# The four loads of layer 1's x become a part of their own in a batch's first step, and the parts of the order stand otherwise

## The reference

```python
xn = layer_norm(x)
q, k, v = xn @ Wq + bq, xn @ Wk + bk, (xn @ Wv + bv) * mask
# layer 0: q = softmax over a head's channels, k = softmax over tokens
y = q @ (k.T @ v)                      # per head
# layer 1:
att = softmax(q @ k.T + (1 - mask) * -1e6, over the keys)
y = att @ v                            # per head
# both:
scale, shift = split(silu(cond) @ W_emb + b_emb)
h = layer_norm(y) * (1 + scale) + shift
x = x + silu(h) @ W_out + b_out
```

## Time and profile before

| | |
|---|---|
| median of three runs | 1425.0 us (1422.28 to 1427.76) |
| profiled execution | 1417.49 us, its span 1415.7 us |
| TensorE busy | 1335.9 us (94%) |
| VectorE, ScalarE, GpSimd busy | 1025.7, 783.6, 771.5 us |
| mean granted clock of TensorE | 0.98 of 2.4 GHz |
| waits of TensorE for a stack | 24.9 us in 22 |

### The profile page before, as it was taken

The page is one execution under the profiler, slowest core; times in us unless marked ns, Lnnn a source line. Parts: engine busy times, 40 slices in busy tenths (PEclk is TensorE's granted clock), DMA queues, the critical chain, the costliest instruction groups (busy, mean ns, idle before and its releaser), DMA issues.

```text
span 1415.7 us, 27902 instructions
## 1 busy us (share of the span) xinstructions
PE 1335.9 (94%) x10720; PEld 1064.4 (75%) x10720; DVE 1025.7 (72%) x2006; ACT 783.6 (55%) x1357; POOL 771.5 (54%) x692
## 2 busy tenths in 40 slices
PE   6899999999999899899999999999999999999888
PEld 4678888888888687577777777776777777777666
DVE  5788878788787876778757757657757757857755
ACT  4355455454554644656755755655755655665642
POOL 0323244332443425468667757748847847856963
PEclk9999999999999999999999999999999999999987
DMA  9021111321213376736436535535635645543602
GB/s 337 2 68 60 38 63 35 97 60 38 66 37 101 96 224 183 212 113 197 133 120 182 147 121 160 161 106 154 190 106 142 180 128 142 169 138 113 187 9 82
DMA packets 83301, 173.40 MB, mean 122 GB/s; under 512 B 7624, under 2 KB 7624, under 8 KB 83168
## 3 DMA queue, kind: packets, MB, share of 16 engines
q1 hardware_dynamic: 83168, 171.62, 40.9%
HBM read 104.45 MB, written 67.14 MB: 121 GB/s over the span
## 4 chain that ended last, share of the span: by engine, by line
PE 59%; DMA 15%; DVE 12%; ACT 6%; SPq 3%; issue 2%; POOL 2%; DVEq 0%; ACTq 0%; POOLq 0%
PE ps L511 11%; PE ps L513 10%; PE ps L512 10%; DMA Ks<-mask_scratch 9%; PE ps L668 7%; PE ps L685 6%; DMA Ks<-stack_scratch 6%; PE ps L726 5%; DVE cT L1188 4%; PE ps L506 4%; ACT ps L784 2%; ACT xTh L782 2%; PE ps L703 2%; PE ps L599 1%; PE ps L620 1%
## 5 line engine op out<-in xcount | busy, mean ns | idle before, releaser
L1363 POOL TENSOR_TENSOR Pb<-Pb 128x512 f32<-128x512 f32 x376 | 470.9, 1292 | 232.4 <-PE ps L726 226.4
L1188 DVE TENSOR_REDUCE cT<-ps 128x1 f32<-128x512 f32 x512 | 325.8, 685 | 134.2 <-PE ps L668 132.1
L926 ACT ACTIVATE Pb<-ps 128x512 f32<-128x512 f32 x512 | 285.8, 599 | 237.5 <-PE ps L685 227.0
L668 PE MATMUL ps<-Ks,Qs 98*128 98x512 f32 x512 | 192.2, 422 | 27.4 <-DMA Ks<-stack_scratch 13.0
L685 PE MATMUL ps<-Qs,Ks 106*128 106x512 f32 x512 | 200.0, 421 | 6.3 <-DVE xTl L1040 3.2
L668 PEld LDWEIGHTS ps<-Ks,Qs 98*128 98x128 f32 x512 | 97.8, 196 | 70.0 <-issue 23.4
L685 PEld LDWEIGHTS ps<-Qs,Ks 106*128 106x128 f32 x512 | 96.9, 192 | 52.2 <-issue 12.9
L1314 POOL TENSOR_TENSOR vt<-vt,qmx 128x512 f32<-128x512 f32 x32 | 33.7, 1055 | 168.2 <-DVE qmx L1105 168.2
L1286 POOL TENSOR_TENSOR rs<-ve,mhalf 128x4 f32<-128x4 f32 x32 | 33.0, 1031 | 156.0 <-DVE ve L1013 126.7
L511 PE MATMUL ps<-xTh,Wh_k 128*128 128x512 f32 x256 | 106.4, 416 | 3.5 <-DVE xTl L1040 2.4
L511 PE MATMUL ps<-Wh_o,sTh 128*128 128x512 f32 x256 | 106.3, 415 | 0.0
(11 more groups left out here) (173 smaller groups left out, 2977.3 us busy)
## 6 DMA issues: line engine op xcount, KB each, us to landing
Qs<-stack_scratch SPq DMA_DIRECT2D x32, 768.0 KB
Ks<-stack_scratch SPq DMA_DIRECT2D x32, 768.0 KB
stack_scratch<-sg_q SPq DMA_DIRECT2D x32, 512.0 KB, 2.7
stack_scratch<-sg_k SPq DMA_DIRECT2D x32, 512.0 KB, 3.0
wr<-in_x SPq DMA_DIRECT2D x32, 256.0 KB, 5.0
x_scratch<-wr SPq DMA_DIRECT2D x32, 256.0 KB, 2.2
stack_scratch<-sg_q SPq DMA_DIRECT2D x32, 256.0 KB, 3.1
stack_scratch<-sg_k SPq DMA_DIRECT2D x32, 256.0 KB, 3.5
```

The lines of the kernel that those rows point to most:

```text
L668: e.matmul(bank[:], Qs[par][0:RX, j, t * 128:(t + 1) * 128], Ks[par][0:RX, j, :], start=True, stop=True).then_inc(s["S"], 1)
L926: e.activation(p_buf(n, m)[:, j, :], ps[bank_of["a", n, m, j]][:], ACT.Exp).then_inc(s["P"], 1)
L1188: e.tensor_reduce(nx[:, n % 2, j, t, 0:1], ps[bank_of["S", n, j, t]][:], AX.X, ALU.max, negate=True).then_inc(s["S_max"], 1)
L1363: e.tensor_tensor(acc[:, j, :], acc[:, j, :], p_buf(n, m)[:, j, :], ALU.add).then_inc(s["Ps_pool"], 1)
```

## The change

The x loads leave `ae` and become the part `lx`, in the first step (g = 0) of the next batch, with marks 0.3 to 0.4. The wait is the same. Besides, many marks of `PLAN` differ, in layer 0 too; of those the diff shows a few.

```diff
-    "0v": ((0.523, 1.2), (0, 0.596)),
+    "0v": ((0.691, 1.2), (0, 0.596)),
...
-    "pv": ((0.365, 0.753, 0.853), (0.338, 0.879, 0.882), (0.466, 1.021, 1.054), (0.328, 0.788, 0.951)),
+    "pv": ((0.365, 0.753, 0.853), (0.338, 0.788, 0.879), (0.466, 1.021, 1.054), (0.328, 0.788, 1.006)),
...
+    "lx": ((0.3, 0.4), None, None, None),
...
+        if g == 0 and b and more:
+            put("lx", [("lx", 8 + b + 1)])
...
-            def ae(i, n):
-                b, g = divmod(n, NG)
-                if g == NG - 1 and b + 2 < B:
-                    e.wait_ge(s["PV"], 4 * n + 4)
-                    for t in range(4):
-                        e.wait_ge(s[f"st{t}"], 16 * (b + 3))
-                    load_x(8 + b + 2)
+            def lx(i, x):
+                e.wait_ge(s["PV"], 16 * (x - 9))
+                for t in range(4):
+                    e.wait_ge(s[f"st{t}"], 16 * (x - 7))
+                load_x(x)
```

More of the change, by code:

```diff
@@ L31 @@
     "st": (0.65,), "sta": (0.0,), "y": (0.3, 0.5, 0.45, 0.45),
-    "qk": MM + (0.3, 0.0), "stack": (0.0,),
+    "qk": MM + (0.3, 0.0), "stack": (0.0,), "lx": (0.0,),
     "S": (0.216,), "nxt": (1.2, 0.3, 0.0),
@@ L42 @@
 PLAN = {
-    "0k": ((0.119, 0.695), (0.405, 1.2)),
-    "0v": ((0.523, 1.2), (0, 0.596)),
+    "0k": ((0.134, 0.71), (0.344, 1.05)),
+    "0v": ((0.691, 1.2), (0, 0.596)),
     "0q": ((0.106, 0.985), (0, 0.247), (0.978, 1.13)),
-    "0o": ((0.012, 1.2), (0, 0.907), (0.06, 0.131)),
-    "att": ((0.155, 0.268, 0.393, 0.585, 0.737), (0.034, 0.211, 0.361, 0.522, 0.66), (0, 0.298, 0.519, 0.672, 0.873), (0, 0.275, 0.306, 0.45, 0.581)),
-    "pv": ((0.365, 0.753, 0.853), (0.338, 0.879, 0.882), (0.466, 1.021, 1.054), (0.328, 0.788, 0.951)),
-    "tl": (None, (0.034, 1.152), (0.157, 0.83), (0, 0.751)),
+    "0o": ((0.012, 0.84), (0, 0.907), (0.06, 0.131)),
+    "att": ((0.155, 0.268, 0.393, 0.585, 0.737), (0.002, 0.187, 0.345, 0.514, 0.66), (0, 0.298, 0.519, 0.672, 0.873), (0.052, 0.275, 0.306, 0.45, 0.581)),
+    "pv": ((0.365, 0.753, 0.853), (0.338, 0.788, 0.879), (0.466, 1.021, 1.054), (0.328, 0.788, 1.006)),
+    "tl": (None, (0.073, 1.091), (0.239, 0.802), (0.102, 0.771)),
     "tlx": ((0.007, 0.513), None, None, None),
-    "ty": ((0, 0.629, 0.766), (0, 0.889, 0.946), (0, 0.899, 0.988), (0, 0.913, 1.05), (1, 0, 0.059)),
-    "S": ((0.405, 0.414, 0.494, 0.654, 0.666), (0.151, 0.322, 0.491, 0.662, 0.834), (0.186, 0.206, 0.601, 0.635, 0.677), (0.211, 0.35, 0.414, 0.511, 0.65)),
-    "nxt": ((0.847, 0.955), (0.899, 0.931), (0.866, 0.886), (0.743, 1.178)),
+    "ty": ((0, 0.629, 0.766), (0, 0.858, 0.946), (0, 0.868, 0.988), (0, 0.965, 1.102), (1, 0, 0.059)),
+    "S": ((0.405, 0.414, 0.494, 0.654, 0.71), (0.151, 0.322, 0.491, 0.662, 0.834), (0.186, 0.206, 0.601, 0.635, 0.677), (0.211, 0.35, 0.414, 0.511, 0.65)),
+    "nxt": ((0.847, 0.955), (0.899, 0.931), (0.866, 0.886), (0.743, 1.188)),
     "q": ((0.057, 0.266, 0.375), (0, 0, 0.02), (0.052, 0.151, 0.269), (0, 0.051, 0.503)),
-    "k": ((0.35, 0.502, 0.539), (0, 0.02, 0.284), (0.13, 0.289, 0.365), (0.082, 0.274, 0.33)),
-    "stack": ((0.701, 0.701), (0.533, 0.533), (0.708, 0.708), (0.955, 0.955)),
+    "k": ((0.351, 0.502, 0.539), (0, 0.02, 0.284), (0.13, 0.289, 0.316), (0.061, 0.264, 0.33)),
+    "stack": ((0.734, 0.734), (0.619, 0.619), (0.807, 0.807), (0.955, 0.955)),
     "nx": (None, (0.012, 0.871), None, None),
     "tx": (None, (0.894, 1.2), None, None),
[2 rows of a table removed]
[2 rows of a table added]
     "we": ((1.2, 1.22), (0.248, 1.104), (0.128, 0.991), None),
[2 rows of a table removed]
[3 rows of a table added]
 }
@@ L1561, in _ @@
             parts = {"w": w, "m": m, "tx": tx, "k": k, "ty": ty, "o": o, "ahead": ahead, "stacks": stacks, "narrow": narrow, "qk": qk,
-                     "stack": stack, "ae": ae, "end": end}
+                     "stack": stack, "lx": lx, "end": end}
             for p, i in order:
```

## The result

The changed kernel takes 1402.7 us (median of four runs, 1401.4 to 1405.0), the kernel before beside it 1426.1 (1422.3 to 1427.8): a ratio of 0.984 [0.982, 0.987], thus 23 us less. The forecast was 1409 with a range of 1402 to 1421; the result lies 0.7 us inside its lower end. The profiled execution of after took 1402.98 us, its span is 1401.2.

A forecast was written before the change was run, and what follows sets the result against it. TensorE, busy 1335.9 of 1415.7 us, was taken as the bound, leaving some 80 us idle to win from. Terms -9.3 - 3.3 - 1.4 - 2.6 - 1.2 + 1.5 = -16.3 took 1425.0 to 1408.7, called 1409; range 1402 to 1421.

The forecast's parts named there:

- Part 1: Batch boundaries in layer 1: with the x loads behind the stack loads on SyncE's queue, the stack lands earlier; -9.3 us.
- Part 2: Without the boundary waits, three falls of TensorE's clock to the lower level go, 1.1 us each; -3.3 us.
- wait 1: S, the first maxima matmul, waits in a batch's first step for the second step's stack; 9.30 us in six waits.
- wait 2: Wait for the third step's stack, some 22 us behind the boundary wait, once in each of the same six batches.
- Part 3: The third-step stack wait's end moves with the boundary wait's; one more 0.23 us matmul ahead fills idle time; -1.4 us.
- the wait moves to wait 2: Rival: something not moving with S holds the third step's stack, so the 9.3 us return there; 1418 us, chance 0.12.
- Part 4: Stack loaded in a batch's third step: its last attention matmul comes two 0.7 us products earlier, ending mask waits; -2.6 us.
- Part 5: Layer 0: two of four El subtractions move to where VectorE idles, shortening TensorE's 2.79 us wait at 462.24; -1.2 us.
- Part 6: Second step: the last S moves behind pv, so the nxs transposes wait about 0.7 us, 0.2 staying per batch; +1.5 us.
- the engines are shared: Rival: transfers share the DMA engines, so the boundary waits and clock falls stay; 1421 us, chance 0.10.
- the slower case: Rival: the wait at L676 is full and grows, with a clock fall each, in all eight batches; 1432 us, chance 0.05.

The follow-up runs named there:

- x move: The kernel before with only the x loads moved into the part lx, all old marks kept: 1411.4 us, ratio 0.991.
- the second of before: The kernel before, unchanged, profiled a second time: median 1425.0 us over 12 runs, the profiled execution 1423.4 us.
- the order with x ahead: The changed kernel with the part lx put ahead of the stack at every boundary, other marks as changed: 1415.9 us, ratio 0.994.
- the fastest kernel: The changed kernel with the wr loads behind the third step's stack and GpSimd's bias additions behind its sTl subtractions (x = 8 to 14): 1394.9 us, ratio 0.979.
- the run before: The changed kernel with the boundary's x loads issued by ScalarE's queue at the start of the first step: 1404.3 us, ratio 0.986.

## Why the prediction was right, and where it was not

**Part 1, x behind the stack (-9.3).** Right: all six waits are gone with x behind the stack in the old order, and most of them come back with x ahead of it in the new. The reason given holds too, that whoever stands ahead in one queue goes first; two queues share.

**Part 2, the clock (-3.3).** Right in kind. The price of 1.1 us a fall between wait 1 and wait 2 took in 0.35 us of transfer time; the fall itself is some 0.75. In the x move TensorE's busy time falls by 2.7 us in the six batches, with two falls in place of four, but about as much came back in wait 2. And the falls of one execution were not the kernel's measure: its runs have a mean clock of 0.977, the profiled one had 0.980, the changed kernel's 0.984. That the x move came out at 13.4 us against 12.6 is in part luck, therefore: against the first profile its six batches are 7.9 us shorter, against the second of before 9.4.

**Part 3, wait 2 (-1.4), "the end of wait 2 moves with wait 1's, and does not eat its gain".** The first half held: from S to the end of wait 2 it is 22.45 us against 22.50. The second did not hold in full in the x move, where wait 2 grew by 2.5 us (9.8 to 12.3) and took what the clock had gained there; the rival "the wait moves to wait 2" came on a small scale. In the changed kernel wait 2 is 4.9 us. Most of the difference is filled, not won: the `nxs` wait of 0.66 and the matmul of 0.23 ahead of it make TensorE come some 0.9 us later, 5 us over six batches.

**Part 4, the third place (-2.6).** Right in mechanism: of the seven mask waits the six in the six batches, 1.8 us, are gone, and the first, 0.83 at 622.56, is still 0.7. Put back in the new order the same marks cost 5 us; the working had the price in the old order, and nothing of what the other parts add to it.

**Part 5, layer 0 (-1.2).** The wait for `El` fell from 2.79 to 1.6, as worked out. But TensorE comes to the first boundary at the same time as before (653.87, against 654.89 - 1.01 = 653.88). The `ql` waits of layer 0 grew from 1.3 us to 2.4, and at the transition, where I looked at no queue, a wait of 2.4 us for `wr` is new while the one for `Wl_q` fell by 1.2. Which of them took the gain isn't shown: without the `wr` wait, with the transition's old marks, the first boundary came at 655.3.

**Part 6, what is added (+1.5).** The wait at L679 in the second step is there, 0.47 us instead of 0.7, and the `xTl` wait of 0.5 behind it is gone, thus nothing instead of 0.2 a batch. A second one, 0.66 in the first step, I did not list: the new order moves the last S of that step back and four transposes ahead of L679 away. It costs little either, because wait 2 stands behind it.

**The sum.** -16.3 became -23: x with its clock 13.3 instead of 12.6, the order 8.8 instead of 3.7. The three traces show where it went in the six batches (us, from the start of the first S to that of the seventh; "before" is the first profile, x move the old marks with the new part):

| | before | x move | after |
|---|---|---|---|
| S, stack with mask | 10.1 | 2.0 | 0 |
| wait 2 | 9.8 | 12.3 | 4.9 |
| `nxs` | 0 | 0 | 6.8 |
| other waits | 3.9 | 4.4 | 1.0 |
| gaps too small to be listed | 2.5 | 2.5 | 2.3 |
| TensorE busy | 622.8 | 620.1 | 617.7 |
| whole | 649.1 | 641.3 | 632.7 |

From the x move to after, the first row is part 4's: 2.0 of 2.6. Parts 3 and 6, set at +0.1 together, came to some -4: wait 2 less 7.4, `xTl` and others less 3.4, `nxs` plus 6.8. The busy time fell by another 2.4 us, most of it likely because the two falls behind the x move's long waits are gone (between orders without a fall it differs by up to 1.3 us); the prediction had this at nothing for the order. The two make up more than the missing 5 us, and parts 4 and 5 fell short by some 2. So the x part was sized about right, the order's gain was not, and the time stayed in the range only just. Of the other rivals, that the engines are shared holds between queues, but x and the stack are in one; nothing of the slower case came.

## What to carry to other kernels

Transfers of one queue are served in its order, so what is read soonest goes ahead, and a load that has time goes behind; but look for that load's first reader on every engine, since moving it without its reader only moved the wait here (1402.7), and moving both won some 8 us (1394.9). A wait whose end is set by a transfer can take in delays ahead of it for nothing, and gains too: split the stretch between two such waits into the engines' part and the transfers' part (here 6.5 and 15 to 17 us) before you count on a faster engine in it. And where an order comes out of marks, print the queue before you say what a mark or a part does: here the new part did nothing that one mark of another track didn't do.

## What was not expected of the hardware

A small operation of VectorE, the 128 x 4 one at L977, takes 0.35 us in the trace of after:

```profile
585.46 0.35 DVE L977 TENSOR_SCALAR be<-cols 128x4 f32<-128x4 f32 x1
```

In two of the fourteen profiled executions (the order with x ahead, and the fastest kernel) it took 7.08 and 6.41 us, at the same place in the program, and TensorE waited 7.7 and 7.0 us for `nxs` behind it:

```profile
585.59 6.41 DVE L977 TENSOR_SCALAR be<-cols 128x4 f32<-128x4 f32 x1
```

These executions took 1424.4 and 1402.0 us, 8.5 and 7.1 above the medians of their kernels. It may be what sets the slow end of other runs; what makes it is open. ScalarE's queue, too, had its first packets only 4 to 5 us after the issue at 959.05, and in the run before 2.5 to 3.5 us after that at 963.44, while SyncE's stack, issued at 958.43, had packets between 959 and 960. Both times q10 began when SyncE's q1 had moved a good part of its stack; whether that held it back was not tried.
